# A decoder layer on one core: the last three iterations of its recurrence in a staggered order, and the third norm's steps moved among its last turns

## What is computed

```python
x = x + attn
ctx = attn.reshape(b * s, d)
xs = _ln(x, g1, b1).reshape(b * s, d)
vs = jnp.zeros_like(xs)

def step(carry, _):
    xs, vs = carry
    u = jnp.tanh(ctx @ w_ctx + xs @ w_x + b_inl)
    vn = vs + DT * (u - xs - vs)
    xn_ = xs + DT * vn
    return ((xn_, vn), None)
(xs, vs), _ = jax.lax.scan(step, (xs, vs), None, length=8)
x = x + xs.reshape(b, s, d)
h = _ln(x, g2, b2)
h = jax.nn.gelu(h @ ff_w1 + ff_b1, approximate=False)
x = x + (h @ ff_w2 + ff_b2)
```

## Time and profile before

| what | value |
|---|---|
| median of 3 runs | 964.28 us |
| the runs | 963.01, 964.28 and 974.3 us |
| the profiled execution's time | 964.21 us |
| its span in the trace | 962.3 us |
| mean granted TensorE clock | 0.963 of full speed |
| PE busy | 881.1 us, 92% |
| DVE, ACT, POOL busy | 577.9, 484.7 and 182.1 us |

### The profile page before, as it was taken

How to read it: one execution, slowest core, us unless ns; L and a number is a source line. 1 busy time by engine, 2 the same in 40 slices (tenths; PEclk the granted TensorE clock), 3 DMA queues, 4 the chain that set the end, 5 groups by cost and what they waited for, 6 DMA issues and landing times. The chain is left out here.

```text
span 962.3 us, 11132 instructions
## 1 busy us (share of the span) xinstructions
PE 881.1 (92%) x3912; PEld 537.6 (56%) x3912; DVE 577.9 (60%) x865; ACT 484.7 (50%) x705; POOL 182.1 (19%) x218
## 2 busy tenths in 40 slices
PE   4889999999999978999999999978676899999997
PEld 3556555545455335444446777744223667777775
DVE  3578757857777125377788764564434556556554
ACT  2423565666666734666656554535534423454332
POOL 9411233133122311000002710000124700000000
PEclk9989999999999988999999999997877999999999
DMA  4042243434434116000000000212755200000000
GB/s 136 14 74 50 41 78 60 82 61 79 99 59 93 22 35 237 0 1 0 1 0 21 1 1 18 48 35 61 144 116 125 86 1 14 10 1 22 0 22 23
DMA packets 22182, 47.39 MB, mean 49 GB/s; under 512 B 7880, under 2 KB 10824, under 8 KB 21744
## 3 DMA queue, kind: packets, MB, share of 16 engines
q1 hardware_dynamic: 19120, 43.17, 20.1%
q0 software_dynamic: 1472, 2.37, 1.3%
q10 hardware_dynamic: 1536, 1.14, 0.5%
HBM read 18.08 MB, written 2.36 MB: 21 GB/s over the span
## 5 line engine op out<-in xcount | busy, mean ns | idle before, releaser
L1140 DVE TENSOR_REDUCE part_max<-psum 128x4 f32<-128x512 f32 x288 | 185.5, 687 | 76.7 <-PE psum L1602 57.6
L856 ACT ACTIVATE prob<-psum 128x1024 f32<-128x1024 f32 (+1 forms) x192 | 145.5, 809 | 85.7 <-PE psum L1624 85.2
L1602 PE MATMUL psum<-k,nat_hi 128*128 128x512 f32 x288 | 119.0, 454 | 6.4 <-DVE part_max L1140 5.0
L1624 PE MATMUL psum<-q,k 128*128 128x512 f32 (+3 forms) x384 | 96.7, 354 | 1.4 <-ACT prob L856 1.4
L1031 ACT ACTIVATE silu<-psum,wt_bias 128x512 f32<-128x512 f32 x64 | 40.5, 684 | 107.6 <-PE psum L355 98.0
L1602 PEld LDWEIGHTS psum<-k,nat_hi 128*128 128x128 f32 x288 | 51.6, 190 | 66.1 <-issue 52.9
L1641 PE MATMUL psum<-prob,vq 128*32 128x512 f32 (+3 forms) x768 | 81.8, 498 | 1.3 <-POOL prob L680 1.2
L680 POOL TENSOR_SCALAR_AFFINE_SELECT prob<-prob 128x256 f32<-128x256 f32 x128 | 52.3, 416 | 155.9 <-ACT prob L856 154.7
L1624 PEld LDWEIGHTS psum<-q,k 128*128 128x128 f32 x384 | 65.0, 189 | 22.5 <-ACT prob L856 11.5
L1478 DVE TENSOR_TENSOR masked_lo<-masked,masked_hi 128x1024 fp32r<-128x1024 f32 x32 | 40.5, 1265 | 40.8 <-ACT masked_hi L1038 40.8
L353 PE MATMUL psum<-masked_hi,wt_hi 128*128 128x512 f32 x128 | 56.1, 438 | 2.6 <-DVE masked_lo L1478 2.1
(11 more groups left out here) (161 smaller groups left out, 1611.0 us busy)
## 6 DMA issues: line engine op xcount, KB each, us to landing
k<-nat_hi SPq DMA_DIRECT2D x92, 64.0 KB, 2.3
xq<-xq_b SPq DMA_DIRECT2D x36, 128.0 KB
q<-nat_hi SPq DMA_DIRECT2D x32, 128.0 KB, 2.3
wt<-in_wt SPq DMA_DIRECT2D x8, 512.0 KB, 4.4
nrm<-in_xT SPq DMA_DIRECT2D x4, 512.0 KB, 5.3
k<-nat_lo SPq DMA_DIRECT2D x32, 64.0 KB, 2.3
q<-nat_lo SPq DMA_DIRECT2D x16, 128.0 KB, 2.4
nrm<-stage SPq DMA_DIRECT2D x32, 64.0 KB, 2.3
```

What stands on the lines that cost most here:

```text
L856: act.activation(prob[:, s % 2, p, :, q0:CH], psum[:, 2 * p:2 * p + 2, q0:CH], ACT.Exp, scale=SCALE)\
L1140: dve.tensor_reduce(part_max[:].rearrange("q (j p i) k -> q p j i k", j=2, p=2)[:, :, :, i, kt], bank(5 + unit_slot[n, u] % 3).rearrange(" ...
L1602: mm = pe.matmul(heads, rounded(nat_hi[:, m, i * P:(i + 1) * P]), k1[:, qd, :, kt * P:(kt + 1) * P], start=True, stop=i != kt)
L1624: mm = pe.matmul(bank(2 * p + j)[:, q0:CH], k2[:, qd, p, j, kt * P:(kt + 1) * P], q2[:, qd, p, c * CH + q0:(c + 1) * CH], start=True, stop ...
```

## The change

The turns of all engines now follow one list, `SCAN`. Iterations 0 to 4 are as before. The last 12 turns, iterations 5, 6 and 7, come in the order (5,0) (5,1) (5,2) (6,0) (5,3) (6,1) (7,0) (6,2) (6,3) (7,1) (7,2) (7,3). The waits are renumbered to suit (`done_at`, `again_at`). Chunk 0 of the norm has its `mean` behind turn (6,3), its `variance` between (7,2) and (7,3) on PE, its `square` behind (7,1) and its `deviation` behind (7,2) on ACT, and its `center`, `total_squares` and `invert` among the last turns of DVE. On ACT, `square(ln3)(1)` now stands behind `third_high(0)`. The pieces of the weights come two at a time behind iterations 1 to 4. GpSimd's additions of `x0` wait for the second tile of FF1 (`ff1_ps`, 2).

```diff
+        SCAN = [(n, c) for n in range(NITER - 3) for c in range(NCH)] + [
+            (NITER - 3 + n, c) for n, c in ((0, 0), (0, 1), (0, 2), (1, 0), (0, 3), (1, 1), (2, 0), (1, 2), (1, 3),
+                                            (2, 1), (2, 2), (2, 3))]
+        AGAIN = [(n, c) for n, c in SCAN if n < NITER - 1]
+
+        def done_at(n, u):
+
+            return 2 * SCAN.index((n, u // 2)) + u % 2 + 1
...
         def pieces_in(n):
 
-            return range(n, min(n + 1, NITER - 1)) if n != NITER - 2 else range(NITER - 2, NITER)
+            return range(2 * n - 2, 2 * n) if 1 <= n <= NITER // 2 else range(0)
...
             pool.wait_ge(x0_in, 16)
+            pool.wait_ge(ff1_ps, 2)
             for c in range(NCH):
                 pool.wait_ge(ln3.d_ready, 2 * (ln3.at + c) + 2)
...
-            for n in range(NITER):
-                for c in range(NCH):
+            for n, c in SCAN:
+                for u in (2 * c, 2 * c + 1):
+                    drive(n, u)
+                if n < NITER - 1:
                     for u in (2 * c, 2 * c + 1):
-                        drive(n, u)
...
+                if (n, c) == (NITER - 1, 1):
+                    square(ln3)(0)
+                if (n, c) == (NITER - 1, 2):
+                    deviation(ln3)(0)
...
-            deviation(ln3)(0)
+            third_high(0)
             square(ln3)(1)
-            third_high(0)
             context_keys()
...
+                if n == NITER - 1 and c < 2:
                     add_state(c)
                     total(ln3)(c)
+                if (n, c) == (NITER - 2, NCH - 1):
+                    center(ln3)(0)
+                if (n, c) == (NITER - 1, 1):
+                    total_squares(ln3)(0)
+                if (n, c) == (NITER - 1, NCH - 1):
+                    invert(ln3)(0)
             center(ln3)(1)
-            invert(ln3)(0)
             scale(ln3)(0)
             total_squares(ln3)(1)
             third_low(0)
...
+            for n, c in SCAN:
+                advance(n, c)
+                if (n, c) == (NITER - 2, NCH - 1):
+                    mean(ln3)(0)
+                if (n, c) == (NITER - 1, 2):
+                    variance(ln3)(0)
             pe.wait_ge(u_ready, UNITS * NITER - 2)
             mean(ln3)(1)
-            variance(ln3)(0)
-
```

More of the change, by code:

```diff
@@ L381, in layer, with again_at @@
         UNITS = 2 * NCH
+        SCAN = [(n, c) for n in range(NITER - 3) for c in range(NCH)] + [
[4 more added lines that the diff above has]
+            return 2 * SCAN.index((n, u // 2)) + u % 2 + 1
+        def again_at(n, u):
+            return 2 * AGAIN.index((n, u // 2)) + u % 2 + 1
         def unit_at(u):
@@ L893, in drive @@
             def drive(n, u):
-                act.wait_ge(z_ps, UNITS * n + 2 * (u // 2) + 2)
+                act.wait_ge(z_ps, done_at(n, u // 2 * 2 + 1))
                 if n > 0:
-                    act.wait_ge(lag_ready, UNITS * (n - 1) + u + 1)
+                    act.wait_ge(lag_ready, again_at(n - 1, u))
                 if n == 0:
@@ L903, in set_context @@
             def set_context(n, u):
-                act.wait_ge(u_ready, UNITS * n + u + 1)
+                act.wait_ge(u_ready, done_at(n, u))
                 act.activation(bank(u), attn_o[:, u % 2, unit_at(u)], ACT.Copy).then_inc(z_set, 1)
-            for n in range(NITER):
-                for c in range(NCH):
+            for n, c in SCAN:
+                for u in (2 * c, 2 * c + 1):
+                    drive(n, u)
+                if n < NITER - 1:
                     for u in (2 * c, 2 * c + 1):
-                        drive(n, u)
[L912 to L917, removed]
-                    act.wait_ge(wff_in, 16)
-                for i in pieces_in(n):
-                    act.activation(rounded(wff_hi[:, piece(i)]), wff[:, piece(i)], ACT.Copy).then_inc(wff_h, 1)
+                        set_context(n, u)
+                if (n, c) == (1, NCH - 1):
+                    act.wait_ge(wff_in, 16)
+                if c == NCH - 1:
+                    for i in pieces_in(n):
+                        act.activation(rounded(wff_hi[:, piece(i)]), wff[:, piece(i)], ACT.Copy).then_inc(wff_h, 1)
+                if (n, c) == (NITER - 1, 1):
+                    square(ln3)(0)
+                if (n, c) == (NITER - 1, 2):
+                    deviation(ln3)(0)
             def third_high(c):
@@ L1240, in add_state @@
                 for m in range(KT):
-                    dve.wait_ge(y_ready, UNITS * NITER + 2 * c + m + 1)
+                    dve.wait_ge(y_ready, UNITS + done_at(NITER - 1, 2 * c + m))
                     at = res[:, m, cols_of(c)]
@@ L1253, in advance @@
                 now, nxt = state(n)[:, u % 2, unit_at(u)], state(n + 1)[:, u % 2, unit_at(u)]
-                dve.wait_ge(u_ready, UNITS * n + u + 1)
+                dve.wait_ge(u_ready, done_at(n, u))
                 if n == 0:
@@ L1257, in advance @@
                 else:
-                    dve.wait_ge(lag_ready, UNITS * (n - 1) + u + 1)
+                    dve.wait_ge(lag_ready, again_at(n - 1, u))
                     dve.scalar_tensor_tensor(nxt, lag[:, u % 2, unit_at(u)], DT - 1, nxt, ALU.mult, ALU.add)\
@@ L1262, in look_back @@
             def look_back(n, u):
-                dve.wait_ge(y_ready, UNITS * (n + 1) + u + 1)
+                dve.wait_ge(y_ready, UNITS + done_at(n, u))
                 dve.scalar_tensor_tensor(lag[:, u % 2, unit_at(u)], state(n + 1)[:, u % 2, unit_at(u)],
@@ L1283, in context_values @@
                                       xvbias[0:CTX, :].rearrange("p (h d) -> p h d", d=HD), ALU.add).then_inc(xv_done, 1)
[L1285 to L1288, removed]
+            for n, c in SCAN:
+                for u in (2 * c, 2 * c + 1):
+                    advance(n, u)
+                if n < NITER - 1:
                     for u in (2 * c, 2 * c + 1):
                         look_back(n, u)
[L1291 to L1301, removed]
+                if c == NCH - 1:
+                    for i in pieces_in(n):
+                        split_low(i)
+                if n == NITER - 1 and c < 2:
                     add_state(c)
                     total(ln3)(c)
+                if (n, c) == (NITER - 2, NCH - 1):
[4 more added lines that the diff above has]
+                    invert(ln3)(0)
             center(ln3)(1)
-            invert(ln3)(0)
             scale(ln3)(0)
@@ L1806, in advance @@
             def advance(n, c):
-                pe.wait_ge(y_ready, UNITS * n + 2 * c + 2)
                 if n == 0:
+                    pe.wait_ge(y_ready, 2 * c + 2)
                     pe.wait_ge(c_ready, 2 * c + 2)
                 else:
-                    pe.wait_ge(z_set, UNITS * (n - 1) + 2 * c + 2)
+                    pe.wait_ge(y_ready, UNITS + done_at(n - 1, 2 * c + 1))
+                    pe.wait_ge(z_set, again_at(n - 1, 2 * c + 1))
                 for m in range(KT):
```

## The result

| | before | after |
|---|---|---|
| median, 20 runs each | 967.62 us | 973.16 us |
| lowest and highest | 962.07, 975.56 | 966.2, 979.13 |
| ratio | 1 | 1.0051, 95% interval 1.0028 to 1.0074 |
| span of the profiled execution | 962.3 us | 976.6 us |
| mean granted clock in it | 0.963 | 0.942 |

The change costs 0.5%, some 5 us (2.7 to 7.2 by the interval; the quotient of the two medians is 1.0057, inside it). The prediction doubted that less than 2% could be told from no change; with 20 executions of each, 0.5% can. The forecast was 4.5 us more, on a level of 964.2; over 20 runs the kernel before lies at 967.6, and so 973.16 lies above the range, which ended at 972.0.

A forecast was written before the change was run, and what follows sets the result against it. The recurrence was taken as bound by PE, with room to win only between its end and FF1. Forecast: 964.2 + 1.3 (FF1 later) + 1.7 (half clock) + 1.5 (additions) = 968.7 us, range 963.0 to 972.0.

The forecast's parts named there:

- the last step: GpSimd's additions among FF1: +1.5 us, shown by a PE wait of 1 to 3 us ahead of chunk 2's variance.
- the anchor of the sum: Whole kernel's starting level: 964.2 us, the profiled execution (span 962.3 and 1.9 around it), with median 964.28.
- Behind it the same waits move along together: Behind the variance of chunk 2: later waits shift together, with no other margin to regain the 1.5 us.
- Stagger and pieces: Recurrence: the staggered turn order and the weight pieces' new places change nothing.
- Last turn: End of the recurrence: variance(0) ahead of the last turn, with a PE wait of 1.5 us, ends the turns +2.4 us.
- From the last turn to FF1: Chain behind the last turn: 8.95 us in place of 10.1, so FF1 starts +1.3 us later.
- Half clock: Start of FF1: after 3.6 us of idle PE, half clock for 3.4 us costs +1.7 us.
- The additions: Among FF1: GpSimd's additions hold DVE, total_squares(2) comes late and PE waits: +1.5 us, bounds 0 and 3.0.
- PE's own lateness: At variance of chunk 2: with FF1 starting at half clock, PE comes 1.7 us late by itself, DVE 3.6 late.
- Table loads: ACT among the tanh turns: two more loads, 1.3 us each, cost nothing by the trace.
- the norm is really off the path: Rival before FF1: FF1 waits for PE alone, starting at 513.0, 4.2 us less; kernel 961.5 us; chance 0.05.

The follow-up runs named there:

- b3: Changed kernel with total_squares(0) first, chunk 0's inverse, scaling and third_low ahead of the last turn's advances on DVE, and spread_out(0) straight behind it on PE: ratio 0.9995.
- c4: Repeat of the kernel with the norm off the path and GpSimd's additions waiting for total_squares(2): ratio 0.9986.
- The filler: Changed kernel with four extra matmuls of 512 columns on PE ahead of FF1, their result overwritten: timed ratio 1.0055.
- b1: Changed kernel with total_squares(0) ahead of add_state(1) and total(1) on DVE: 965.97 us in one run; timed again, ratio 1.0036.
- b4: Kernel with the norm off the path, with GpSimd's additions waiting for total_squares(2) in place of FF1's second tile: ratio 1.0007.
- c2: The changed kernel again, unaltered: timed ratio 1.0063 to the kernel before.
- d1: Changed kernel with total_squares(0) ahead of add_state(1) on DVE and square of chunk 1 ahead of third_high(0) on ACT: ratio 1.0015.
- e1: Repeat, timed, of the changed kernel with total_squares(0) ahead of add_state(1) and total(1) on DVE: ratio 1.0036.
- e2: Repeat, timed, of the changed kernel with four extra matmuls on PE in the wait ahead of FF1: ratio 1.0055.
- e3: Repeat, timed, of the changed kernel with the square of chunk 1 ahead of third_high(0) on ACT again: ratio 1.0012.
- a4: Staggered order and new places of the weight pieces alone; norm's steps and GpSimd's additions as before the change: 961.08 us in one run.
- a1: Changed kernel with the square of chunk 1 ahead of third_high(0) on ACT again: 967.59 us in one run.
- a3: Changed kernel with four extra matmuls on PE ahead of FF1, their result overwritten: 971.91 us in one run.
- a2: Changed kernel without GpSimd's wait for FF1's second tile, additions starting when center(0) has read its chunk: 975.02 us in one run.

## Why the prediction was wrong

**The difference was right, partly by luck, and three of its four steps were seen as forecast.** Forecast +4.5 us; the marks give +4.45 up to the end of the block, and the timings 4.9 (2.7 to 7.2). But +1.3, +1.7 and +1.5 were measured as +0.88, +2.45 and +1.10: errors of -0.4, +0.75 and -0.4 that cancel. And the sign of the last step, a wait of 1 to 3 us ahead of variance(2), did not come: it was 0.18.

**The step that failed is the anchor of the sum**: "964.2 (the profiled execution; ... the median is 964.28) + 1.3 + 1.7 + 1.5 = 968.7 us". I took three runs of 963.01 to 974.3 us for a level known to a tenth. Over 20 runs it was 967.62, 3.3 higher, and 967.6 + 4.5 = 972.1 is 1 us from what was measured. Without that error the forecast would have been off by the 1 us alone, for which the next paragraphs have only an open explanation. The range held the bounds of the local costs and nothing for the level of the runs.

**What made the level uncertain** lies outside the touched stretch: over all profiles 392.8 to 401.9 us ahead of the recurrence, and 326.8 to 340.3 us from the block's end to the end, with PE at half clock for more or less of the cross-attention. Of the kernel before and of the changed one, windows in that stage:

```profile
680.00:700.00 20.00, 13.15 (x67) 5.70 (x66) 8.31 (x21) 9.90 (x13) 3.00 (x5) 0.81 0.78 139
700.00:720.00 20.00, 13.89 (x46) 5.90 (x44) 8.20 (x13) 5.34 (x8) 4.25 (x5) 0.76 0.56 113
```

```profile
680.00:700.00 20.00, 17.30 (x61) 8.06 (x60) 8.37 (x19) 9.38 (x12) 2.43 (x4) 0.64 0.79 160
700.00:720.00 20.00, 14.56 (x47) 6.06 (x46) 7.27 (x15) 7.44 (x9) 1.80 (x3) 0.50 0.70 124
```

**"Behind it the same waits move along together"** was too sure. What the marks give as a ratio is the difference of the block's ends over 967. In seven of nine timed comparisons the measured ratio lies 0.5 to 3.3 parts in a thousand above that, in two (b3, c4) 0.3 and 1.8 below; the quotients of the medians have the same signs. The filler's lower end, 1.0035, excludes its 1.0022, b1's, 1.0011, its 1.0006, and b4's, 0.9982, its 0.9974. So in some of these orders 1 to 3 us seem to come behind the block, or the block itself is longer in executions that were not profiled, as c4 shows for b4.

Of the first the traces show a sign. Over the 120 us behind the block's end the mean granted clock is 0.82 and 0.76 in the two profiles of the kernel before, and 0.69, 0.66 and 0.68 in the three of the changed one (0.67 to 0.82 in the other twelve); the first profile of each:

```profile
635.12:755.12 120.00, 88.96 (x369) 45.02 (x368) 54.18 (x99) 56.24 (x68) 26.08 (x26) 0.82 0.52 111
639.60:759.60 120.00, 98.91 (x355) 48.81 (x354) 52.19 (x97) 54.22 (x64) 23.23 (x23) 0.69 0.50 107
```

The timed executions agree: the median of their mean clocks was 0.9475 in c2 against 0.957 of the kernel before beside it, and it was lower too in b4 (0.953 against 0.956), c4, d1, e1, e2 and e3, while in b3, one of the two with no excess, it was higher (0.961 against 0.956). So the changed order goes with more half clock behind the block. Whether the clock falls there because the stretch ahead ends at another time, as at FF1 in b1, was not tried, and how much of the 1 to 3 us it makes stays open. The profiled executions of the changed kernel (978.32, 980.89 and 976.49 us) were also slower than its median.

The terms, one by one:
- *Stagger and pieces, nothing*: 0.1 us or less (a4). Right.
- *Last turn, +2.4*: 509.37 - 507.05 = 2.3. PE's wait is 1.11 by its row, where I had 1.5. Right; b1 takes it away and wins 1.37.
- *From the last turn to FF1, 8.95*: 518.08 - 509.37 = 8.71, by the chain as I had it. FF1 +0.9 in place of +1.3. The swap of square and `third_high` was put at 1.9 and measured at 1.82 (a1).
- *Half clock, +1.7*: 2.45 (a3). It came as said and lasted twice as long, almost 7 us in place of 3.4: under-sized. At half clock the variance took 1.70 us in place of 0.95, and ACT's root and Gelu waited for it.
- *The additions, +1.5*: 1.10 where FF1 runs at full clock (a3, a1), with a wait of 0.75 at variance(2), and a wait of only 0.18 where it does not: at half clock DVE idled and let them pass. The step that I had wrong here is PE's own lateness. Counted from FF1's start, `total_squares(2)` ends 3.85 us later than before, where I had 3.6, but PE by itself comes 3.27 later (538.80 - 518.08 against 534.60 - 517.15), where I had 1.7, and so it hardly waits. The two costs are therefore not independent. a2 has the half clock and the early additions: 246.31 - 125.18 = 121.13 us from FF1 to the block's end, against 121.52 in the changed kernel and 117.95 before. So the additions cost 0.4 at half clock and 1.10 at full clock, and the half clock 3.2 without them and 2.45 with them. Both together make 3.57, in place of 3.2.
- *Table loads, nothing*: tanh(7,3) started at 509.56, 1.75 us after ACT was free, and the three loads took 1.28 us each. Behind the first the next operation followed at once; behind the other two ACT waited for PE. The Trainium skill, "ScalarE: Activation LUTs", section "What ACT_TABLE_LOAD costs", has a drain of about 1.4 us beside it; these rows show none: square root 0.01 us behind its load, load 0.03 behind the root. The measurement decides.
- *The rival "the norm is really off the path"* needed another order than the change wrote; b3 has it, and FF1 came at 116.7, where that rival said 513.0 - 396.3 = 116.7.

## What to carry to other kernels

When a step is moved ahead of a chain, look at what stands before each of its successors in the queues: here the early square root bought nothing, as its inverse stood behind the last advances, and a square put one line later held the chain by 1.8 us. A wait on PE costs itself and then may cost the clock. It can be filled, shortened or moved, and all three kept the clock up in the profiles; but in the timing only the shorter one came back to the level before (1.0012, against 1.0055 for the filled and 1.0036 for the moved). And when a kernel's single runs differ by more than the change is worth, put the spread of the runs into the range, and judge the change by marks inside the trace.

## What the runs showed that I had not expected

Two waits of PE of 3.57 us each, in programs that differ in the place of one DVE operation, ended in half clock in three of three profiles and in full clock in two of two; the one began 1.4 us sooner behind the same work. A third program with such a wait, a2, fell in its one profile. Waits of 2.87 us (a2) and 2.59 (b3) were followed by a fall, those of 1.75 (a1, e3, d1) were not, and the wait of 2.3 us in one and the same program ended in full clock in b4 and in half clock in c4. So the length of a wait does not decide alone; where it lies may, and in b4 and c4 the outcome differed from execution to execution. And half clock in FF1 did not only slow PE, it let GpSimd's additions run in DVE's idle time: the wait at variance(2) fell from 0.75 to 0.18 us.
